# Loops written out, attention heads side by side on the two halves of the array, and the first pass's causal mask added inside VectorE's maximum

## The reference

```python
def attention(x, ...):                      # B=8, T=512, C=128, H=16, D=8
    q, k, v = heads(wq, bq), heads(wk, bk), heads(wv, bv)
    q, k = rope(q), rope(k)
    att = einsum('bhtd,bhsd->bhts', q, k) / sqrt(D)
    att = softmax(where(causal, att, -inf))
    return merge(einsum('bhts,bhsd->bhtd', att, v)) @ wp.T + bp
...
for round in (a, b):
    x = x + attention_of_round(layernorm(x))
    x = x + mixture(layernorm(x))           # 8 heads of 64, softmax without a mask, experts
```

## Time and profile before

| what | value |
|---|---|
| median of 3 runs | 2208.72 us (2204.95 to 2209.61) |
| the profiled execution | 2209.6 us, its span 2207.9 us |
| PE busy | 1899.7 us, 86% of the span |
| DVE busy | 1637.4 us, 74% |
| ACT busy | 1275.3 us, 58% |
| POOL busy | 1045.1 us, 47% |
| mean granted clock of PE | 0.945 of full |

### The profile page before, as it was taken

One profiled execution on the slowest core, in us unless ns is written; L12 is line 12 of the kernel. 1 busy time (PEld: TensorE's weight loads), 2 busy tenths in 40 slices (PEclk: granted clock), 3 DMA queues, 4 the chain that ended last, 5 costly groups with the idle time before them and its releaser, 6 DMA issues.

```text
span 2207.9 us, 40511 instructions
## 1 busy us (share of the span) xinstructions
PE 1899.7 (86%) x11328; PEld 913.1 (41%) x11328; DVE 1637.4 (74%) x2950; ACT 1275.3 (58%) x2803; POOL 1045.1 (47%) x1124
## 2 busy tenths in 40 slices
PE   1758998899898889989888998989899898998775
PEld 0323444435354443535444353544434354443433
DVE  4548787877878787787878777787877777796561
ACT  0326657575665757566575756657575665757452
POOL 1214455462635546263554626355462635555433
PEclk8779999999999999999999999999999999999977
DMA  3121212020121202012120201212020121200000
GB/s 95 42 34 30 34 40 35 28 34 17 34 34 40 34 28 35 16 35 33 40 34 28 36 16 36 31 40 34 28 37 21 34 28 39 34 6 13 10 10 5
DMA packets 87623, 68.19 MB, mean 31 GB/s; under 512 B 10720, under 2 KB 83104, under 8 KB 87328
## 3 DMA queue, kind: packets, MB, share of 16 engines
q1 hardware_dynamic: 87456, 66.62, 16.5%
HBM read 32.51 MB, written 10.49 MB: 19 GB/s over the span
## 4 chain that ended last, share of the span: by engine, by line
PE 49%; DVE 29%; issue 12%; ACT 5%; DMA 2%; POOL 1%; DVEq 1%; SPq 0%; ACTq 0%; POOLq 0%; PEldq 0%; PEld 0%
DVE nmaxA L878 6%; PE Y L488 6%; PE S1c L429 4%; DVE ztmp L999 4%; DVE nmaxF L883 4%; PE S1b L429 4%; PE S2a L453 4%; PE M L619 3%; PE S2b L453 3%; PE Y L479 3%; PE S1a L429 3%; DVE rotated L924 2%; PE M L539 2%; ACT Pq L713 2%; PE M L592 2%
## 5 line engine op out<-in xcount | busy, mean ns | idle before, releaser
L1117 POOL TENSOR_TENSOR Z<-Z,ztmp 128x1280 f32<-128x1280 f32 x112 | 324.8, 2900 | 374.7 <-DVE ztmp L999 373.5
L1084 POOL TENSOR_SCALAR_AFFINE_SELECT PT<-PT 128x256 f32<-128x256 f32 (+1 forms) x640 | 248.3, 400 | 395.8 <-ACT PT L698 393.1
L1108 POOL TENSOR_TENSOR Vf<-Vf,ztmp 128x512 f32<-128x512 f32 x256 | 352.5, 1377 | 139.9 <-DVE ztmp L973 134.8
L698 ACT ACTIVATE PT<-S2a 128x512 f32<-128x512 f32 x320 | 191.1, 597 | 152.7 <-PE S2a L447 124.4
L488 PE MATMUL Y<-PT,Vf 128*64 128x512 f32 x1024 | 274.8, 617 | 0.0
L429 PE MATMUL S1a<-Kf,Qf 64*128 64x512 f32 x352 | 216.6, 698 | 6.6 <-ACT Pq L713 4.6
L973 DVE TENSOR_TENSOR ztmp<-xv,wv_s 128x512 f32<-128x512 f32 x256 | 219.7, 858 | 2.8 <-POOL Z L1117 2.8
L429 PE MATMUL S1c<-Kf,Qf 64*128 64x512 f32 x352 | 209.2, 676 | 12.6 <-ACT Pq L713 11.2
L702 ACT ACTIVATE PT<-S2a 128x512 f32<-128x512 f32 x256 | 153.1, 598 | 89.8 <-PE S2a L453 89.6
L698 ACT ACTIVATE PT<-S2b 128x512 f32<-128x512 f32 x320 | 191.3, 598 | 14.1 <-PE S2b L447 13.2
L429 PE MATMUL S1b<-Kf,Qf 64*128 64x512 f32 x320 | 190.8, 678 | 6.5 <-ACT Pq L713 6.5
(11 more groups left out here) (109 smaller groups left out, 3931.5 us busy)
## 6 DMA issues: line engine op xcount, KB each, us to landing
Qs<-parts SPq DMA_DIRECT2D x96, 128.0 KB
Ks<-parts SPq DMA_DIRECT2D x96, 128.0 KB
tab_s<-in_tab SPq DMA_DIRECT2D x16, 512.0 KB, 4.3
xr<-out_x SPq DMA_DIRECT2D x32, 256.0 KB, 2.8
out_x<-res SPq DMA_DIRECT2D x32, 256.0 KB, 2.2
wa_s<-in_wa SPq DMA_DIRECT2D x16, 320.0 KB, 2.9
xl<-out_x SPq DMA_DIRECT2D x16, 256.0 KB, 2.8
out_x<-in_x SPq DMA_DIRECT2D x8, 256.0 KB, 4.7
```

What stands on the lines that cost most here:

```text
L698: nc.scalar.activation(PT[:, slot % 2, b, :], t[:, :], ACT.Exp, scale=SCALE_A).then_inc(exps_done.sem, 1)
L1084: last = nc.gpsimd.affine_select(out=v, in_=v, compare_op=ALU.is_ge, fill=0.0, base=0, pattern=pattern, channel_multiplier=-1)
L1108: nc.gpsimd.tensor_tensor(Vf[:, i, :, :], Vf[:, i, :, :], vtmp[:, n % VBUF, :, :], ALU.add).then_inc(v_acc.sem, 1)
L1117: nc.gpsimd.tensor_tensor(Z[:, :, :, :], Z[:, :, :, :], ztmp[:, hh % 2, :, :, :], ALU.add).then_inc(z_acc.sem, 1)
```

## The change

Three things change together. The loop of turns 3 to 15 is written out on every engine, and the small instructions that kept waits apart (`apart`) go. The heads of the causal attention lie side by side: the even heads' parts of q and k at rows 0 to 49 (the maxima at 48 and 49) of `Qs` and `Ks`, the odd heads' at rows 64 to 113, so a matmul of either pass takes 48 or 50 rows of one half of the array; both passes fill two banks per even step b, one for an even and one for an odd head, and wait until both banks are free. The mask matmul goes: DVE adds the mask (`maskw`, 384 zeros and then the triangle) and takes the maximum in one `tensor_tensor_reduce` per head and block of queries, which also writes the masked scores back into the bank. The parts of q and k go to `Qs` and `Ks` in 24 DMAs per unit and not 12, of half the size.

```diff
-    ROWS_P1 = 96
+    ROWS_P1 = NSP * DA
     ROWS_P2 = ROWS_P1 + 2
+    HALF = 64
...
-    for pair in range(GA // 2):
-        h0, h1 = 2 * pair, 2 * pair + 1
-        for h in (h0, h1):
-            BANKS_A1 += [[(h, 3, 0)], [(h, 2, 0), (h, 0, 384)]]
-            BANKS_A2 += [[(h, 0, 0)], [(h, 1, 0), (h, 3, 384)]]
-        BANKS_A1.append([(h0, 1, 0), (h1, 1, 256)])
-        BANKS_A2.append([(h0, 2, 0), (h1, 2, 256)])
+    for h0 in range(0, GA, 2):
+        BANKS_A1 += [[(h, 3, 0)] for h in (h0, h0 + 1)] + [[(h, 2, 0), (h, 0, 384)] for h in (h0, h0 + 1)]
+        BANKS_A2 += [[(h, 0, 0)] for h in (h0, h0 + 1)] + [[(h, 1, 0), (h, 3, 384)] for h in (h0, h0 + 1)]
+    BANKS_A1 += [[(h, 1, 0), (h + 2, 1, 256)] for h in (0, 1)]
+    BANKS_A2 += [[(h, 2, 0), (h + 2, 2, 256)] for h in (0, 1)]
...
                         for r in range(NSP):
-                            sp.dma_start(dst[DA * r:DA * r + DA, :, :],
-                                         parts[:, qk, order[r], :]).then_inc(scattered.sem, 16)
+                            for lo in (0, HALF):
+                                sp.dma_start(dst[lo + DA * r:lo + DA * r + DA, :, :],
+                                             parts[lo:lo + HALF, qk, order[r], :]).then_inc(scattered.sem, 16)
...
# pass1, on PE
-                    if group >= SA and b % GF:
+                    if b % 2:
                         return
...
-                    pe.wait_ge(*s1_free(j, (n if group < SA else n + 1) - len(S1)))
+                    pe.wait_ge(*s1_free(j, n + 1 - len(S1)))
                     if group < SA:
-                        for h, qt, col in BANKS_A1[b]:
-                            hh, keys = GA * group + h, (qt + 1) * P
-                            nc.tensor.matmul(t[:, col:col + keys], Qs[0:ROWS_P1, hh, qt * P:keys],
-                                             Ks[0:ROWS_P1, hh, 0:keys], start=True, stop=False)
-                            last = nc.tensor.matmul(t[:, col + qt * P:col + keys], identb[:, :], maskb[:, :],
-                                                    start=False, stop=True)
-                        last.then_inc(s1_filled.sem, 1)
+                        for i in range(2):
+                            for h, qt, col in BANKS_A1[b + i]:
+                                hh, keys, r = GA * group + h, (qt + 1) * P, HALF * (h % 2)
+                                last = nc.tensor.matmul(S1[(n - 1 + i) % len(S1)][:, col:col + keys],
+                                                        Qs[r:r + ROWS_P1, hh // 2, qt * P:keys],
+                                                        Ks[r:r + ROWS_P1, hh // 2, 0:keys], start=True, stop=True)
+                            last.then_inc(s1_filled.sem, 1)
...
# pass2, on PE
-                    pe.wait_ge(exps_done.sem, exps_done.at(j, n - len(S2)))
+                    pe.wait_ge(exps_done.sem, exps_done.at(j, (n + 1 if slot < SA else n) - len(S2)))
...
# maxima, on DVE
                     if group < SA:
-                        segs = BANKS_A1[b]
-                        h0, qt0, _ = segs[0]
-                        if len(segs) == 2 and segs[1][1] == qt0:
-                            last = nc.vector.tensor_reduce(nmaxA[:, GA * group + h0:GA * group + h0 + 2, qt0],
-                                                           t[:, :].rearrange("p (h k) -> p h k", h=2), AX.X, ALU.max,
-                                                           negate=True)
-                        else:
-                            for h, qt, col in segs:
-                                last = nc.vector.tensor_reduce(nmaxA[:, GA * group + h, qt:qt + 1],
-                                                               t[:, col:col + (qt + 1) * P], AX.X, ALU.max, negate=True)
+
+                        for h, qt, col in BANKS_A1[b]:
+                            keys = (qt + 1) * P
+                            last = nc.vector.tensor_tensor_reduce(
+                                t[:, col:col + keys], t[:, col:col + keys], maskw[:, T - keys:T], 1.0, -3.0e38,
+                                ALU.add, ALU.max, maxA[:, h % 2, GA // 2 * group + h // 2, qt:qt + 1])
                         last.then_inc(s1_read.sem, 1)
...
# on every engine
-            for j in range(HEAD):
-                iteration(j, **parts_of(j))
-            with dve.Fori(HEAD, UNITS) as j:
-                iteration(j, **ALL)
-            for j in range(UNITS, LAST):
+            for j in range(LAST):
                 iteration(j, **parts_of(j))
```

More of the change, by code:

```diff
@@ L71, in pb @@
             return ctx.enter_context(nc.psum_tensor(name, [P, 512], dt))
-        waits_passed = {e: ctx.enter_context(nc.semaphore(f"waits_passed_{n}")) for n, e in
-                        (("sp", nc.sync), ("pool", nc.gpsimd), ("dve", nc.vector), ("pe", nc.tensor))}
-        def apart(eng):
-            eng.sem_inc(waits_passed[eng], 1)
         class Signal:
@@ L315, in rows @@
                     sp.wait_ge(*drained(j, f"rows{group}"))
-                    apart(sp)
-                    for i in range(2):
-                        sp.dma_start(Qs[ROWS_P1 + i:ROWS_P1 + i + 1, GA * group:GA * group + GA, :],
-                                     mrowA[i * GA * NT:(i + 1) * GA * NT, :]).then_inc(rowsA_in.sem, 16)
+                    for odd in range(2):
+                        r = HALF * odd + ROWS_P1
+                        sp.dma_start(Qs[r:r + 2, GA // 2 * group:GA // 2 * (group + 1), :],
+                                     mrowA[odd * GA * NT:(odd + 1) * GA * NT, :]).then_inc(rowsA_in.sem, 16)
                 if f_end:
                     sp.wait_ge(resA_ready.sem, resA_ready.at(j, 1, 2))
-                    apart(sp)
                     sp.dma_start(xr[:, :, :], stream(j - 3)).then_inc(xrF_loaded.sem, 16)
@@ L434, in pass2 @@
                     t = S2[(n - 1) % len(S2)]
+                    if slot < SA and b % 2:
+                        return
                     if not (a if slot < SA else f):
@@ L442, in pass2 @@
                         pe.wait_ge(rowsA_in.sem, rowsA_in.at(j, 2 * slot + 2, 1))
[L443 removed]
+                    pe.wait_ge(exps_done.sem, exps_done.at(j, (n + 1 if slot < SA else n) - len(S2)))
                     if slot < SA:
[L445 to L448 removed]
+                        for i in range(2):
+                            for h, kt, col in BANKS_A2[b + i]:
+                                hh, r = GA * slot + h, HALF * (h % 2)
+                                last = nc.tensor.matmul(S2[(n - 1 + i) % len(S2)][:, col:col + T - kt * P],
+                                                        Ks[r:r + ROWS_P2, hh // 2, kt * P:kt * P + P],
+                                                        Qs[r:r + ROWS_P2, hh // 2, kt * P:T], start=True, stop=True)
+                            last.then_inc(s2_filled.sem, 1)
                     else:
@@ L668, in iteration @@
                             f_output()
-            for j in range(HEAD):
-                iteration(j, **parts_of(j))
-            with pe.Fori(HEAD, UNITS) as j:
-                iteration(j, **ALL)
-            for j in range(UNITS, LAST):
+            for j in range(LAST):
                 iteration(j, **parts_of(j))
@@ L683, in _ @@
             nc.scalar.activation(identb[:, :], ident[:, :], ACT.Copy).then_inc(consts_cast.sem, 1)
-            nc.scalar.activation(maskb[:, :], maskf, ACT.Copy).then_inc(consts_cast.sem, 1)
             def iteration(j, a, f, f_end, a_prep, f_prep):
@@ L795, in iteration @@
                                                  ACT.Exp, scale=-1.0).then_inc(sig_e.sem, 1)
-            for j in range(HEAD):
-                iteration(j, **parts_of(j))
-            with act.Fori(HEAD, UNITS) as j:
-                iteration(j, **ALL)
-            for j in range(UNITS, LAST):
+            for j in range(LAST):
                 iteration(j, **parts_of(j))
@@ L1142, in iteration @@
                             f_mix((slot - 2) % NS - SA, b // 2 - 1, 3 if slot < 2 else 2)
-            for j in range(HEAD):
-                iteration(j, **parts_of(j))
-            with pool.Fori(HEAD, UNITS) as j:
-                iteration(j, **ALL)
-            for j in range(UNITS, LAST):
+            for j in range(LAST):
                 iteration(j, **parts_of(j))
@@ L1160 @@
     H, D = 16, C // 16
-    plain = [h * D + d for d in range(D) for h in range(H)]
-    swapped = [h * D + (d + D // 2) % D for d in range(D) for h in range(H)]
+    plain = [h * D + d for odd in range(2) for d in range(D) for h in range(odd, H, 2)]
+    swapped = [h * D + (d + D // 2) % D for odd in range(2) for d in range(D) for h in range(odd, H, 2)]
     def layout(wq, wk, wv, wp, bq, bk, bv, bp):
```

67 lines of the change are left out of this document (24 added, 43 removed).

## The result

| what | before | after |
|---|---|---|
| median | 2208.7 us (2204.95 to 2209.61) | 2235.9 us (2233.54 to 2237.49, 4 runs) |
| ratio to before | 1 | 1.0126, 95% interval 1.0108 to 1.0143 |
| span of the profiled execution | 2207.9 us | 2234.7 us |
| mean granted clock of PE | 0.945 | 0.916 |

The account below looks back on a forecast made before the run. DVE was taken to bound the kernel from mid slot 6 through slot 1 of the next turn. Per turn 4 x 2.2 - 3.6 = +5.3 us, +84 over 16 units, loop -28: +56, 2265 us; 8-in-10 range 2180 to 2350.

Parts of the forecast that it names:

- The loop: Turns 4 to 15: the loop's branch costs 2.33 us, 12 times, so writing it out saves 28 us.
- Rival 4: Written-out turns bring nothing, as the branch's cost comes back elsewhere: 2293 us, chance 0.05.
- What bounds each slot: DVE sets the pace in slots 7, 0 and 1; PE bounds slot 2 and, until it gives way, slot 6.
- The pair on DVE: First pass, slots 6, 7, 0, 1: maximum plus write-out cost 0.20 us per pair beyond columns, +2.2 us per group.
- The low end: Lower bound for the DVE pair: fixed costs 0.07 + 0.07 us, so +1.3 us per group.
- What PE sheds: Slots 6, 7, 0, 1: less PE work can only close DVE's waits for scores, -3.6 us per turn.
- The halves' overlap: Matmuls on both halves overlap only partly, saving PE 0.68 us per group and pass; full overlap 1.13.
- Slots 2 and 3: PE sheds 0.68 us each, but second-pass pairs wait for both banks; taken as nothing, bounds -0.7 and +0.7 each.
- The sum: Per turn +5.3 us, over 16 units +84; with the loop's -28, +56 us in all.
- Rival 1: The DVE pair is cheap, under 0.144 us, and the kernel gets faster: about 2196 us, chance 0.20.
- Rival 2: DVE's columns go at half speed in the new maximum: 337 us more, 2600 us, chance 0.06.
- Rival 3: DVE newly waits for PE's pairs, or PE's clock falls, in slots 7, 0, 1: +40, 2305 us, chance 0.19.

Follow-up runs that it names:

- e7: The changed kernel with the first pass issued ahead of the second in slots 2 and 3; 2181.71 us, ratio 0.9889.
- e4: The kernel before with the loop written out and the mask added on DVE, heads and banks as before; 2203.83 us, ratio 0.9979.
- e1: The kernel before with the loop of turns 3 to 15 written out, nothing else; 2175.28 us, ratio 0.9872.
- e11: e1 with the first pass issued ahead of the second in slots 2 and 3, single banks kept; 2171.38 us, ratio 0.9827.
- e9: The changed kernel with single second-pass banks in slots 2 and 3 only; three executions 2222.1 to 2223.8 us, one 2182.8.
- e2: The changed kernel with its second pass filling one bank per step, first pass still paired; 2196.17 us, ratio 0.9956.
- e10: e7 with the mask back on PE, in matmuls on the score's own half, and the plain maximum on DVE; 2176.68 us, ratio 0.9850.
- e12: The changed kernel with the edits of e2 and e7 together; 2193.75 us, ratio 0.9928.
- e13: e10 with the second pass filling one bank at a time; 2181.49 us, ratio 0.9885.

## Why the prediction was right in sign, by luck, and wrong in size

Two steps failed, with opposite signs: the fixed cost of the pair on DVE was put too high, and the wait for a pair of second-pass banks in slots 2 and 3 was put at nothing. The kernel got slower, as forecast, only through the second. Without its 41 us the time would be some 14 us under that of the kernel before (an estimate, 27 - 41), and e7, which mends most of it, is faster than before.

- **The loop** (-28): right, -33 measured alone. Rival 4 is out.
- **What bounds each slot**: right. DVE fills slots 7, 0 and 1, and putting the heads on halves brought nothing there: e4 needs 63.06 us for slots 6, 7, 0 and 1 together, the changed kernel 63.02.
- **The pair on DVE** (+2.2 us per group): this is the first step that failed, "For the write-out: ... DVE's small ones are nearest: 0.07". The next instruction starts with the write-out, and the pair as a whole has some 0.10 us beyond its columns where the sum had 0.20. So by the medians a group takes 4 x (0.62 + 0.48 + 0.38 + 0.25) = 6.9 us, +0.7 where the sum had +2.2. The low end, 0.14 per pair, was still too high, and the forecast's own sign of being wrong, a pair under 0.15 us, came true. DVE's busy time rose by 33 us in all where 142 were forecast. The figure was borrowed from the smallest DVE instructions, since no row of before showed such a pair.
- **What PE sheds** (-3.6): in the turn shown, slots 6, 7, 0 and 1 with 62.86 us for e1's 61.40 hold 59.38 us of DVE for 55.60. DVE has 3.8 more, its idle time fell by 2.3 (the sum had 3.6), and +1.5 remains where the sum had +5.3. Not all of the 3.8 is the pairs, 4 x 0.7: in the means of turns 4 to 15 DVE is busy 1.8 us less in slots 2 and 3 than in e1, so a part is work of the mixture that has moved ahead into slot 1.
- **The halves' overlap**: the step by which only 128 or 256 columns of a bank with two blocks overlap failed; the overlap is full. That changed little, since the changes of the tiling, which no step had, take it back in slot 6: 1.0 of 1.13 us per group.
- **Slots 2 and 3** ("I take nothing there", bounds -0.7 and +0.7 each): the second step that failed. They cost +1.75 and +0.83 over e1, 2.6 us per turn, 41 us. The forecast saw that a pair waits for both banks, but didn't ask who is queued behind the wait: the mixture's scores, for which DVE and ACT wait. e7 shows it.
- **The sum**: over e1, by the table, slots 6, 7, 0 and 1 have +1.62 us, slots 2 and 3 +2.58, slot 4 -0.37. Sixteen times, +26 + 41 - 6, and -33 for the loop, make +28; measured +27. The two wrong terms had opposite signs: slots 6, 7, 0 and 1 too dear by 84 - 26 = 58 us, slots 2 and 3 too cheap by 41. That the sum was off by only 29 us is luck.
- **Rival 1** had its condition met (a pair under 0.144 us), and yet the kernel got slower: the rival had slot 2 gain 0.7 us, and it lost 1.8. With slot 2 mended (e7) it is 2182 us, faster than before, but over e1's 2175. **Rival 2** is out. **Rival 3** named a new wait, but in the first pass; there PE was not late. The waits of DVE for PE fell from 4.1 us per turn in e1 to 1.4 in slots 6, 7, 0 and 1. The lower clock came: slot 1 went from 0.80 to 0.69 in turn 8 and from a mean of 0.87 to 0.70. It cost little in slot 1 itself (16.24 us, 16.41 before and 16.00 in e1), as DVE fills it. It isn't what made the change slow: e7 has the same mean in slot 1 (0.69) and takes 54 us less.
- What stays open: how much of each later difference is the clock in slots 1, 3 and 4. The means over 12 turns mix turns like the two shown for e11, and e9 shows one program at two times, as far apart as e2 and the changed kernel. So of e2's 40 us the clock may have a part; e7's 54 us have the same clock on both sides. Differences of 5 to 12 us among e7, e10, e12 and e13 can't be given to one cause, and those of 5 us may be none.
